# A long-convolution kernel with adapters: order of the stores and of the first tiles' moments in its preparation

## The chip, the cores and the metric

The kernel runs on one core of a Trainium2 chip. The metric is the device time of one execution in microseconds (us); three runs of the kernel before gave a median of 2400.53 us.

## The reference

The input x has 8 sequences of 2048 rows with 512 channels. Two layers follow one another, each with a layer norm in front and a residual behind:

```python
x = x + hyena(layernorm(x))      # first layer
x = x + adapters(layernorm(x))   # second layer
# hyena(x):
proj = (x @ in_proj_w + in_proj_b).reshape(B, L, C, 3)
v = depthwise_conv3(proj[..., 0], short_w) + short_b
h = gelu(pos @ fw1 + fb1); h = gelu(h @ fw2 + fb2)       # pos: 2048 positions from 0 to 1
coefs = (h @ fw3 + fb3).reshape(L, C, 2)                 # only order 1 reaches the output
conv = irfft(rfft(v, 2L) * rfft(coefs[..., 1], 2L))[:L]  # along the sequence, per channel
return (proj[..., 2] * conv) @ out_w + out_b
# adapters(x): x @ (sum over 8 ids of weight * W[id]).T, plus the mixed bias
```

The filter, that is coefs of order 1, doesn't depend on x. It is computed once and used for all 8 sequences. All is float32.

## The kernel before

The program has four stages, one behind the other, and each begins when all engines have left the stage before it. `prep` makes the filter, its partial spectrum and the split weights. `front` normalizes x, projects it and makes the first step of the transform. `middle` makes the rest of the transform, the product and the way back. `back` gates, projects and applies the adapters. The change touches `prep` alone, and beside it one more scratch slice (`fc["spare"]`, L1448).

`prep` has a program for each engine and one for the queue on SyncE (SP). They run in parallel and meet only at semaphores.

- **Loads.** SP issues 17 loads in a fixed order (L280 to L297). The small network waits for the first five of them (`net_in`), the per-row tables `ramp` and `short_w` raise `rows_in`, and `in_proj_w` comes in four blocks of 128 rows, two of them ahead and two within the loop, because `wraw` has two buffers.
- **The network.** ScalarE (ACT) and TensorE (PE) make `h2` from `pos` (L356, L416, L361). VectorE (DVE) cuts fw3 and fb3 (L488 to L493), corrects the low parts of the bias (L502, L505) and makes the running sums of `h2` by a scan (L509). PE's loop begins when it has `bias_low` from L505.
- **The first tiles' moments.** Between L493 and L502 DVE waits for x's first four tiles and makes their mean and variance (L496, L499). GpSimd (POOL) makes the factors from them with a power (L326 to L331) ahead of all its other work, and ACT normalizes tiles 0 and 1 (L371) ahead of its loop.
- **The loop.** It has iterations e = 0 to 19 for 16 tiles of 128 rows. In iteration e PE makes filter rows e (L433, L437), running sums e-1 (L447, L452) and the transform of tile e-4 (L465). DVE multiplies the filter rows by the three taps and adds them (L519, L523, L531, L536, L541). ACT copies sums e-1 to `e1` (L378) and the transform of e-4 to `s1o` (L384); in some iterations it also rounds a block of weights (L395, L396) or of the matrix (L402), whose low part POOL makes (L341, L342, L336).
- **The stores.** SP runs over tiles t, not over iterations. For each t it waits for the third tap and stores `gy` (L300), waits for the sums and stores `e1` (L302), and waits for the transform and stores `s1o` (L304). Behind tiles 1 and 3 it waits for POOL and loads a block of weights (L309).
- **The buffers.** `gy` has 4, `e1` 3, `s1o` 2, `gx` 2, `g` 5, and each of the three PSUM pairs 2. The waits on them are these:

```python
# ACT, e1_copy(t)
act.wait_ge(e1_stored[t % 3], 16 * (t // 3))   # t >= 3
# ACT, s1_copy(t)
act.wait_ge(s1_stored[t % 2], 16 * (t // 2))   # t >= 2
# DVE, third tap of tile t
dve.wait_ge(e0_stored[t % 4], 16 * (t // 4))   # t >= 4
# PE, filter_rows(e), sums(t), stage1(t)
pe.wait_ge(tap2, e - 3); pe.wait_ge(e1_done, t - 1); pe.wait_ge(s1_out, t - 1)
```

At the end SP waits for loads only, not for its last stores.

Of the kernel before, what the change touches and what calls it, by code (L numbers as in the profile page):

```python
# [10 lines left out]
ALU = mybir.AluOpType  # L11
ACT = mybir.ActivationFunctionType
# [9 lines left out]
T = 16  # L22
# [8 lines left out]
SUB = 4  # L31
# [133 lines left out]
def hyena_adapter_kernel(nc, x, in_w, in_b, short_w, short_b, fw1, fb1, fw2, fb2, fw3, fb3,  # L165
# [21 lines left out]
    def prep(fc, mc):  # L187
        with ExitStack() as st:
# [8 lines left out]
            GR = 5  # L197
            LAG = 4
            W_AT = (1, 2, 9, 12)
            W_LOAD_AT = (1, 3)  # L200
            S1_AT = (5, 6, 7, 8)
            BIAS_AT = 4

# [11 lines left out]
            pos = wide[0:64]  # L215
# [25 lines left out]
            net_in = sem("p_net_in")  # L241
# [33 lines left out]
            def edge_rows(q, t):  # L275
                return edge_f[q][:, t * C:(t + 1) * C]

            @block.sync
            def _(sp):
                sp.dma_start(w1c[:], fw1.rearrange("a (p b) -> p (a b)", b=1)).then_inc(net_in, 16)  # L280
                sp.dma_start(b1c[:], fb1.rearrange("(p b) -> p b", b=1)).then_inc(net_in, 16)
                sp.dma_start(pos, consts["pos"].partition_broadcast(64)).then_inc(net_in, 16)
                sp.dma_start(w2s[:], fw2).then_inc(net_in, 16)
                sp.dma_start(b2c[:], fb2.rearrange("(p b) -> p b", b=1)).then_inc(net_in, 16)
                sp.dma_start(b3r, fb3.rearrange("(a n) -> a n", a=1).partition_broadcast(2 * BR)).then_inc(w3_in, 16)
                sp.dma_start(w3, fw3).then_inc(w3_in, 16)
                sp.dma_start(sbr[:], short_b.rearrange("(a c) -> a c", a=1).partition_broadcast(P)).then_inc(sb_in, 16)
                for h in range(2):
                    sp.dma_start(fc["xg0"][h * N1:(h + 1) * N1], by_tile(x[0])[h, :, 0:SUB, :]).then_inc(fc["x_in"][0], 16)
                sp.dma_start(ramp, consts["ramp"].partition_broadcast(2 * BR)).then_inc(rows_in, 16)  # L290
                sp.dma_start(tapr, short_w.rearrange("(o c) a w -> o (c a w)", o=1).partition_broadcast(P)).then_inc(rows_in, 16)
                for kt in range(2):
                    sp.dma_start(wraw[:, kt], in_w[kt * P:(kt + 1) * P, :]).then_inc(w_in[kt], 16)
                sp.dma_start(s1, consts["s1"]).then_inc(mats_in, 16)
                sp.dma_start(s1x[:], consts["s1x"]).then_inc(mats_in, 16)
                sp.dma_start(bv3[:], in_b.rearrange("(a c) -> a c", a=1).partition_broadcast(P)).then_inc(mats_in, 16)
                sp.dma_start(fc["ident"][:], consts["ident"]).then_inc(mats_in, 16)  # L297
                for t in range(T):
                    sp.wait_ge(tap2, t + 1)
                    sp.dma_start(edge_rows(0, t), gy[:, t % 4]).then_inc(e0_stored[t % 4], 16)  # L300
                    sp.wait_ge(e1_done, t + 1)
                    sp.dma_start(edge_rows(1, t), e1[:, t % 3]).then_inc(e1_stored[t % 3], 16)  # L302
                    sp.wait_ge(s1_out, t + 1)
                    sp.dma_start(spec_f.rearrange("(r h t) c -> t r h c", h=2, t=T)[t], s1o[:, t % 2]).then_inc(s1_stored[t % 2], 16)  # L304
                    if t in W_LOAD_AT:

                        kt = 2 + W_LOAD_AT.index(t)
                        sp.wait_ge(w_low, 2 * (kt - 1))
                        sp.dma_start(wraw[:, kt % 2], in_w[kt * P:(kt + 1) * P, :]).then_inc(w_in[kt % 2], 16)  # L309
                sp.wait_ge(mats_in, 64)  # L310

            @block.gpsimd
            def _(pool):
                pool.memset(inside[:], 1.0 / BR).then_inc(zeroed, 1)
                pool.memset(h2[:, 0:1], 0.0).then_inc(zeroed, 1)
                pool.memset(h2[:, LP - 1:LP], 0.0).then_inc(zeroed, 1)
                pool.wait_ge(zeroed, 3)
                pool.memset(inside[:, 0, 0:1], 0.0).then_inc(zeroed, 1)
                pool.memset(inside[:, 1, P - 1:P], 0.0).then_inc(zeroed, 1)
                pool.memset(fc["power"], -0.5).then_inc(fc["power_set"], 1)  # L320
                pool.memset(fc["eps"], EPS).then_inc(fc["power_set"], 1)
                pool.memset(fc["minus"], -1.0).then_inc(fc["power_set"], 1)
                pool.wait_ge(fc["power_set"], 3)
                r, m = fc["rstd"][:, 0], fc["shift"][:, 0]
                pool.wait_ge(fc["mv_done"], SUB)
                pool.tensor_tensor(r, fc["mv"][:, 0, :, 1], fc["eps"], ALU.add).then_inc(fc["pow_step"], 1)  # L326
                pool.tensor_tensor(m, fc["mv"][:, 0, :, 0], fc["minus"], ALU.mult).then_inc(fc["pow_step"], 1)
                pool.wait_ge(fc["pow_step"], 2)
                pool.tensor_tensor(r, r, fc["power"], ALU.pow).then_inc(fc["pow_step"], 1)
                pool.wait_ge(fc["pow_step"], 3)  # L330
                pool.tensor_tensor(m, m, r, ALU.mult).then_inc(fc["norm_ready"], 1)  # L331

                def s1_lows(k):
                    part = slice(k * (T // 4), (k + 1) * (T // 4))
                    pool.wait_ge(s1_high, k + 1)
                    pool.tensor_tensor(fc["s1l"][:, part], s1[:, part], fc["s1h"][:, part].bitcast(F32), ALU.subtract).then_inc(s1_low, 1)  # L336

                def w_lows(kt):
                    rows = wraw[:, kt % 2].rearrange("p (c w) -> p c w", w=3)
                    pool.wait_ge(w_high, 2 * kt + 2)  # L340
                    pool.tensor_tensor(fc["wvl"][:, kt], rows[:, :, 0], fc["wvh"][:, kt].bitcast(F32), ALU.subtract).then_inc(w_low, 1)  # L341
                    pool.tensor_tensor(fc["wgl"][:, kt], rows[:, :, 2], fc["wgh"][:, kt].bitcast(F32), ALU.subtract).then_inc(w_low, 1)  # L342

                w_lows(0)
                w_lows(1)
                for k in range(4):
                    s1_lows(k)
                w_lows(2)
                w_lows(3)

            @block.scalar
            def _(act):
# [13 lines left out]
                        act.activation(b3ehl[:], b3e[:], ACT.Copy).then_inc(bias_high, 1)  # L366
                act.wait_ge(rows_in, 32)
                act.activation(ramp_r[:], ramp, ACT.Copy).then_inc(masks, 1)
                act.wait_ge(fc["norm_ready"], 1)
                for t in range(2):  # L370
                    act.activation(fc["xn"][:, t], fc["xg0"][:, t], ACT.Identity, bias=fc["shift"][:, 0, t:t + 1],  # L371
                                   scale=fc["rstd"][:, 0, t:t + 1]).then_inc(fc["xn_done"], 1)

                def e1_copy(t):
                    act.wait_ge(c_ps, t + 1)
# [10 lines left out]
                for e in range(T + LAG):  # L386
# [4 lines left out]
                    if e in W_AT:  # L391
                        kt = W_AT.index(e)
# [6 lines left out]
                    if e in S1_AT:  # L399
                        k = S1_AT.index(e)  # L400
                        part = slice(k * (T // 4), (k + 1) * (T // 4))
                        act.activation(fc["s1h"][:, part], s1[:, part], ACT.Copy).then_inc(s1_high, 1)  # L402
                    if e == BIAS_AT:
                        act.wait_ge(mats_in, 64)
                        bias = bv3[:].rearrange("p (c w) -> p w c", w=3)
                        act.activation(fc["bvr"][:], bias[:, 0], ACT.Copy)
                        act.activation(fc["bgr"][:], bias[:, 2], ACT.Copy)

            @block.tensor
            def _(pe):  # L410
# [75 lines left out]
            def _(dve):  # L486
# [4 lines left out]
                dve.wait_ge(sliced, 2)  # L491
                dve.tensor_tensor(b3e[:], b3s[:], sbr[0:2 * BR], ALU.mult).then_inc(sliced, 1)
                dve.tensor_tensor(w3e[:], w3s[:], sbr[:], ALU.mult).then_inc(sliced, 1)  # L493
                dve.wait_ge(fc["x_in"][0], 32)
                for i in range(SUB):
                    dve.bn_stats(fc["stats"][:, 0, i], fc["xg0"][:, i]).then_inc(fc["bn_step"], 1)  # L496
                dve.wait_ge(fc["bn_step"], SUB)
                for i in range(SUB):
                    dve.bn_aggr(fc["mv"][:, 0, i], fc["stats"][:, 0, i]).then_inc(fc["mv_done"], 1)  # L499
                low = slice(BR, 2 * BR)  # L500
                dve.wait_ge(bias_high, 1)
                dve.tensor_tensor(b3hl[low], b3s[low], b3hl[low].bitcast(F32), ALU.subtract).then_inc(bias_low, 1)  # L502
# [10 lines left out]
                for e in range(T + 2):  # L513
# [12 lines left out]
                    if e >= 2:  # L526
                        t = e - 2
# [9 lines left out]
                    if e >= 2:  # L537
                        t = e - 2
                        dve.wait_ge(tap01, t + 1)
                        dve.wait_ge(tap2, t + 1)  # L540
                        dve.tensor_tensor(g[:, t % GR], g[:, t % GR], gy[:, t % 4], ALU.add).then_inc(g_done, 1)  # L541

    def front(fc, mc):
        with ExitStack() as st:
# [888 lines left out]
    with ExitStack() as st:  # L1433
# [11 lines left out]
        fc["stats"] = small[:, 0:48].rearrange("p (s i k) -> p s i k", s=2, i=SUB)  # L1445
        fc["mv"] = small[:, 48:64].rearrange("p (s i k) -> p s i k", s=2, i=SUB)
        fc["rstd"], fc["shift"] = (small[:, 64 + 8 * k:72 + 8 * k].rearrange("p (s i) -> p s i", s=2) for k in range(2))
        fc["power"], fc["eps"], fc["minus"] = (small[:, 80 + SUB * k:80 + SUB * (k + 1)] for k in range(3))  # L1448
        for name in ("power_set", "bn_step", "mv_done", "pow_step", "norm_ready", "xn_done"):
            fc[name] = sem("f_" + name)  # L1450
        both = ExitStack()
# [62 lines left out]
```

## Time and profile before

| | |
|---|---|
| three runs | 2394.57, 2400.53, 2400.6 us |
| profiled execution | 2403.85 us |
| its span | 2402.0 us, granted clock 0.985 |
| PE busy | 2315.6 us (96%) |
| DVE busy | 1530.5 us (64%) |
| ACT busy | 843.9 us (35%) |
| POOL busy | 933.0 us (39%) |
| DMA | 496.60 MB, mean 207 GB/s |

The span is the time from the first to the last instruction, and lies 1.85 us below the device time of the same execution. The busy shares are means over all four stages. The page cuts the span in 40 slices of 60 us; the digits of PE over the first three are 6, 6 and 8, and 9 in nearly all others. `prep` takes the first 132 us. The granted clock is the share of TensorE's full clock (2.4 GHz) that a stretch had; 0.5 would be 1.2 GHz all through.

### The profile page before, as it was taken

The page shows a single profiled execution, that of the slowest core. Times are in us where ns is not written, and L with a number is a line of the kernel's source. Part 1 is how long each engine was busy: PE and PEld are TensorE (multiplying, and loading weights), DVE is VectorE, ACT ScalarE, POOL GpSimd, SP SyncE. Part 2 cuts the span into 40 slices and gives each one's busy share as a digit, 9 for nine tenths or more (in the row PEclk, how much of TensorE's full clock was granted, in tenths as well). Part 3 has the DMA queues.
Part 4 walks back from the last instruction along what each step waited for, and adds up shares of the span by engine and source line. Part 5 has one row for each costly group of instructions (what it writes and reads, how often), then busy time and mean ns, then how long its engine had stood idle before and what let it go on. Part 6 is the DMA issues. An engine that isn't in the chain of part 4 may idle for free.

```text
span 2402.0 us, 39735 instructions
## 1 busy us (share of the span) xinstructions
PE 2315.6 (96%) x12804; PEld 1624.1 (68%) x12804; DVE 1530.5 (64%) x2180; ACT 843.9 (35%) x1152; POOL 933.0 (39%) x1182
## 2 busy tenths in 40 slices
PE   6689999999999999999999979999999999999998
PEld 2267777777777777644444426777777777777776
DVE  5534444443434444367777757888888888888886
ACT  3234444444444444344444432222222222222222
POOL 2122222222222222100000026777777777777774
PEclk9889999999999999999999999999999999999999
DMA  5545545555444546589999997766665665666563
GB/s 187 181 137 159 196 140 179 162 164 196 150 162 146 188 160 221 205 312 359 356 353 355 362 358 229 246 178 176 176 180 175 179 175 176 178 179 177 177 179 101
DMA packets 180517, 496.60 MB, mean 207 GB/s; under 512 B 19419, under 2 KB 19740, under 8 KB 159332
## 3 DMA queue, kind: packets, MB, share of 16 engines
q1 hardware_dynamic: 150756, 395.10, 51.4%
q10 hardware_dynamic: 29696, 100.68, 11.6%
q8 instruction: 35, 0.57, 0.1%
q14 instruction: 30, 0.25, 0.0%
HBM read 276.27 MB, written 219.43 MB: 206 GB/s over the span
## 4 chain that ended last, share of the span: by engine, by line
PE 53%; DVE 2%; issue 2%; DMA 1%; ACT 0%; DVEq 0%; POOL 0%; POOLq 0%; SPq 0%
PE m_psW L1030 7%; PE m_psA L1013 6%; PE b_psF L183 5%; PE b_psC L1328 5%; PE b_psF L184 5%; PE b_psO L184 5%; PE b_psF L185 5%; PE b_psO L183 5%; PE b_psO L185 5%; PE b_psP L1342 2%; PE b_psT L1359 2%; DVE m_m L1101 2%; DMA spec<-wide_out 0%; DMA b_fin<-spec 0%; DVE b_o L1397 0%
## 5 line engine op out<-in xcount | busy, mean ns | idle before, releaser
L1101 DVE TENSOR_TENSOR m_m<-m_psA,m_spec 128x1024 f32<-128x1024 f32 x256 | 295.5, 1215 | 114.8 <-PE m_psA L1013 113.1
L758 POOL TENSOR_TENSOR vl<-v,vh 128x512 fp32r<-128x512 f32 x128 | 165.2, 1291 | 390.1 <-ACT vh L716 390.1
L1292 ACT ACTIVATE b_zh<-b_psT 128x512 fp32r<-128x512 f32 x128 | 76.5, 597 | 636.9 <-PE b_psT L1359 636.9
L1030 PE MATMUL m_psW<-m_m,mats 64*64 64x512 f32 x2048 | 256.0, 591 | 2.5 <-issue 2.5
L1013 PE MATMUL m_psA<-m_xin,mats 64*64 64x512 f32 x1536 | 212.9, 601 | 9.5 <-DVE m_m L1101 5.9
L183 PE MATMUL psV<-wvh,nth 128*128 128x512 f32 x512 | 213.6, 417 | 0.6 <-DVE ntl L840 0.6
L859 DVE TENSOR_TENSOR gto<-psG,bgr 128x512 f32<-128x512 f32 x128 | 87.5, 684 | 195.4 <-PE psG L185 195.2
L183 PE MATMUL b_psO<-woh,b_oh 128*128 128x512 f32 x512 | 211.8, 414 | 0.0
L183 PE MATMUL b_psF<-wfh,b_zh 128*128 128x512 f32 x512 | 207.7, 406 | 2.8 <-DVE b_zl L1421 2.8
L840 DVE TENSOR_TENSOR ntl<-psT,nth 128x512 fp32r<-128x512 f32 x128 | 88.1, 688 | 178.9 <-ACT nth L710 178.9
L184 PE MATMUL b_psO<-wol,b_oh 128*128 128x512 f32 x512 | 201.4, 393 | 0.0
L184 PE MATMUL b_psF<-wfl,b_zh 128*128 128x512 f32 x512 | 201.2, 393 | 0.0
L185 PE MATMUL b_psO<-woh,b_ol 128*128 128x512 f32 x512 | 201.2, 393 | 0.0
L184 PE MATMUL psV<-wvl,nth 128*128 128x512 f32 x512 | 201.0, 393 | 0.0
L716 ACT ACTIVATE vh<-v 128x512 fp32r<-128x512 f32 x128 | 80.9, 632 | 341.2 <-DVE v L852 341.2
L185 PE MATMUL psV<-wvh,ntl 128*128 128x512 f32 x512 | 200.6, 392 | 0.0
L185 PE MATMUL b_psF<-wfh,b_zl 128*128 128x512 f32 x512 | 200.0, 391 | 0.0
L185 PE MATMUL psG<-wgh,ntl 128*128 128x512 f32 x512 | 199.5, 390 | 0.0
L183 PE MATMUL psG<-wgh,nth 128*128 128x512 f32 x512 | 199.2, 389 | 0.0
L184 PE MATMUL psG<-wgl,nth 128*128 128x512 f32 x512 | 199.2, 389 | 0.0
L1065 ACT ACTIVATE wide_out<-m_psW 128x1024 f32<-128x1024 f32 x128 | 130.8, 1022 | 192.6 <-PE m_psW L1030 192.5
L1030 PEld LDWEIGHTS m_psW<-m_m,mats 64*64 64x64 f32 x2048 | 113.6, 134 | 111.2 <-issue 90.1
(136 smaller groups left out, 4685.3 us busy)
## 6 DMA issues: line engine op xcount, KB each, us to landing
spec<-wide_out SPq DMA_DIRECT2D x64, 1024.0 KB, 9.0
spec<-wide_out ACTq DMA_DIRECT2D x64, 1024.0 KB, 9.2
b_fin<-spec SPq DMA_DIRECT2D x128, 512.0 KB, 4.6
m_xin<-spec SPq DMA_DIRECT2D x30, 2048.0 KB, 11.7
xg<-in_L_attn_x_dram SPq DMA_DIRECT2D x64, 512.0 KB, 6.2
gate_d<-gto SPq DMA_DIRECT2D x32, 1024.0 KB, 4.0
b_gin<-gate_d SPq DMA_DIRECT2D x128, 256.0 KB, 3.6
b_xin<-in_L_attn_x_dram SPq DMA_DIRECT2D x256, 128.0 KB, 3.2
```

What stands on the lines that cost most here:

```text
L183: pe.matmul(out_ps, w_hi, d_hi, start=first, stop=False)
L184: pe.matmul(out_ps, w_hi, d_lo, start=False, stop=False)
L185: return pe.matmul(out_ps, w_lo, d_hi, start=False, stop=last)
L716: act.activation(vh[:, t % 2], v[:, t % 2], ACT.Copy).then_inc(v_hi, 1)
L758: pool.tensor_tensor(vl[:, t % 2], v[:, t % 2], vh[:, t % 2].bitcast(F32), ALU.subtract).then_inc(v_lo, 1)
L840: dve.tensor_tensor(ntl[:, t % 2], psT[t % 2][:].rearrange("p (k r) -> p k r", k=CT), nth[:, t % 2].bitcast(F32), ALU.subtract).then_inc(n ...
L859: dve.tensor_tensor(gto[:, slot, t % SUB], psG[:], bgr[:], ALU.add).then_inc(g_out, 1)
L1013: mm = pe.matmul(psA[k % RA][half[q], slot, :], w[half[slot]], xin[half[slot], par, B if k < 2 else 2 * (k - 2) + q, :], start=True, stop= ...
L1030: mm = pe.matmul(psW[pair % 2][half[slot], q, :], ws[slot][half[q]], m[half[q], pair % RM, part, slot, :], start=part == 0, stop=part == 1)
L1065: act.activation(wo[:, par, 2 * pair:2 * pair + 2, :], psW[pair % 2][:], ACT.Copy).then_inc(w_out, 1)
L1101: dve.tensor_tensor(m[:, (k - 2) % RM, part], psA[k % RA][:], spec[:, par, part], ALU.mult).then_inc(m_done, 1)
L1328: mm = pe.matmul(psC[t % 2][h * N1:(h + 1) * N1, :], s4[:, h * T + t, :], fin[:, t % 2, h, :], start=True, stop=True)
```

## The change

SP issues its stores by iteration: in iteration e the sums of tile e-1, the transform of tile e-4 and the third taps of tile e-2. The two loads of weights come behind the stores of iterations 3 and 6. `pos` is loaded ahead of `w1c` and `b1c`. The moments (DVE), their factors (POOL) and the two normalizations (ACT) stand behind all other work of their engines in `prep`. POOL makes one power on constants into a scratch slice, right behind its memsets.

```diff
-            W_LOAD_AT = (1, 3)
+            W_LOAD_AT = (3, 6)
@@ SP
+                sp.dma_start(pos, consts["pos"].partition_broadcast(64)).then_inc(net_in, 16)
                 sp.dma_start(w1c[:], ...)
                 sp.dma_start(b1c[:], ...)
-                sp.dma_start(pos, consts["pos"].partition_broadcast(64)).then_inc(net_in, 16)
...
-                for t in range(T):
+                def store_taps(t):
                     sp.wait_ge(tap2, t + 1)
                     sp.dma_start(edge_rows(0, t), gy[:, t % 4]).then_inc(e0_stored[t % 4], 16)
+                def store_sums(t):
                     sp.wait_ge(e1_done, t + 1)
                     sp.dma_start(edge_rows(1, t), e1[:, t % 3]).then_inc(e1_stored[t % 3], 16)
+                def store_spectrum(t):
                     sp.wait_ge(s1_out, t + 1)
                     sp.dma_start(spec_f..., s1o[:, t % 2]).then_inc(s1_stored[t % 2], 16)
-                    if t in W_LOAD_AT:
-                        kt = 2 + W_LOAD_AT.index(t)
+                for e in range(T + LAG):
+                    if 1 <= e <= T:
+                        store_sums(e - 1)
+                    if e >= LAG:
+                        store_spectrum(e - LAG)
+                    if 2 <= e < T + 2:
+                        store_taps(e - 2)
+                    if e in W_LOAD_AT:
+                        kt = 2 + W_LOAD_AT.index(e)
                         sp.wait_ge(w_low, 2 * (kt - 1))
                         sp.dma_start(wraw[:, kt % 2], ...).then_inc(w_in[kt % 2], 16)
@@ POOL: this is new; the factors (four operations from the wait on mv_done on) move behind w_lows(3)
+                pool.tensor_tensor(fc["spare"], fc["eps"], fc["power"], ALU.pow)
@@ ACT: from behind ramp_r to behind the loop
+                act.wait_ge(fc["norm_ready"], 1)
+                for t in range(2):
+                    act.activation(fc["xn"][:, t], fc["xg0"][:, t], ACT.Identity, ...).then_inc(fc["xn_done"], 1)
@@ DVE: from behind w3e to behind the loop
+                dve.wait_ge(fc["x_in"][0], 32)
+                for i in range(SUB):
+                    dve.bn_stats(fc["stats"][:, 0, i], fc["xg0"][:, i]).then_inc(fc["bn_step"], 1)
+                dve.wait_ge(fc["bn_step"], SUB)
+                for i in range(SUB):
+                    dve.bn_aggr(fc["mv"][:, 0, i], fc["stats"][:, 0, i]).then_inc(fc["mv_done"], 1)
```

## Rows read from the trace of the kernel before

**Rows 1.** Busy us by stretch: PE, PEld, DVE, ACT, POOL; granted clock, DMA share, GB/s

```profile
34.00:48.40 14.40, 14.22 (x59) 5.73 (x60) 14.40 (x21) 8.05 (x11) 5.13 (x4) 1.00 0.30 110
84.48:120.79 36.31, 24.53 (x75) 7.96 (x75) 20.94 (x28) 10.63 (x14) 2.80 (x2) 0.83 0.46 174
```

**Rows 2.** Longest wait of the preparation: total us, times, longest

```profile
ACT m_xin L378 <- DMA edge_f<-m_xin: 56.1, 12, 8.4
```

**Rows 3.** Timeline, one slow iteration: start us, duration, engine, line, idle before

```profile
108.69 0.60 ACT L378 ACTIVATE m_xin<-pE 128x512 f32<-128x512 f32 x1 [4.54 <-DMA edge_f<-m_xin]
109.18 1.02 ACT L384 ACTIVATE m_xin<-pS 128x1024 f32<-128x1024 f32 x1
110.22 0.55 SPq L304 DMA_DIRECT2D spec_f<-m_xin  x1
111.47 0.83 SPq L302 DMA_DIRECT2D edge_f<-m_xin  x1
114.74 0.60 ACT L378 ACTIVATE m_xin<-pE 128x512 f32<-128x512 f32 x1 [4.54 <-DMA edge_f<-m_xin]
```

**Rows 4.** Timeline, DVE's first tap in iterations 2, 5 and 7

```profile
34.00 0.88 DVE L519 TENSOR_TENSOR g<-pA,m_xin 128x512 f32<-128x512 f32 x1 [3.79 <-PE pA L437]
...
44.92 0.84 DVE L519 TENSOR_TENSOR g<-pA,m_xin 128x512 f32<-128x512 f32 x1
...
51.86 0.83 DVE L519 TENSOR_TENSOR g<-pA,m_xin 128x512 f32<-128x512 f32 x1
```

**Rows 5.** Timeline, from the network to the first iterations

```profile
7.26 2.93 ACT L356 ACTIVATE wide<-wide,b1c,w1c 64x512 f32<-64x512 f32 x4 [5.25 <-DMA b2c<-in_L_attn_fb_dram]
...
15.42 0.69 ACT L361 ACTIVATE h<-pA,b2c 128x512 f32<-128x512 f32 x1 [0.69 <-PE pA L416]
17.55 2.47 DVE L496 BATCH_NORM_STATS2 f_small<-xg 128x6 f32<-128x512 f32 x4 [3.46 <-DMA xg<-in_L_attn_x_dram]
...
21.07 0.68 DVE L505 TENSOR_TENSOR b3ehl<-b3e,b3ehl 32x512 fp32r<-32x512 f32 x1
...
21.67 1.91 ACT L368 ACTIVATE ramp_r<-wide_out 64x2048 fp32r<-64x2048 f32 x1 [5.57 <-DMA m_xin<-in_L_attn_short_w_dram]
21.78 4.42 DVE L509 TENSOR_TENSOR_SCAN wide<-h 128x2048 f32<-128x2048 f32 x1
...
27.35 1.52 ACT L371 ACTIVATE xn<-xg,f_small 128x512 f32<-128x512 f32 x2 [3.77 <-POOL f_small L331]
...
29.07 0.79 PE L452 MATMUL pE<-b3ehl,ramp_r 64*128 64x512 f32 x1
```

**Rows 6.** Timeline, last store of the preparation and first work of front

```profile
130.89 0.55 SPq L304 DMA_DIRECT2D spec_f<-m_xin  x1
...
132.13 1.94 PE L770 MATMUL psT<-fident,xn 128*128 128x128 f32 x8 [5.03 <-PEq L188]
```

**Rows 7.** Timeline, DVE, the moments of tiles 4 to 7 in front

```profile
140.48 2.46 DVE L829 BATCH_NORM_STATS2 f_small<-xg 128x6 f32<-128x512 f32 x4
143.10 0.38 DVE L836 BATCH_NORM_AGGREGATE f_small<-f_small 128x2 f32<-128x6 f32 x4 [0.15 <-DVE f_small L829]
```

**Rows 8.** Timeline, POOL, the last factor of the same tiles

```profile
145.08 0.20 POOL L754 TENSOR_TENSOR f_small<-f_small 128x4 f32<-128x4 f32 x1
```

**Rows 9.** Line L329, the first power: ns min/median/max, first and last start

```profile
L329 POOL TENSOR_TENSOR f_small<-f_small x1: 5142/5142/5142, 21.9 to 21.9; 128x4 f32<-128x4 f32 x1
```

**Rows 10.** Timeline, PE at the low clock, sums of two iterations

```profile
73.04 1.98 PE L447 MATMUL pE<-w3e,wide 128*64 128x512 f32 x4 [6.26 <-ACT m_xin L378]
...
79.58 1.91 PE L447 MATMUL pE<-w3e,wide 128*64 128x512 f32 x4
```

**Rows 11.** Line L304, all 16 stores, from issue

```profile
DMA to landing us min/median/max: 3.1/3.1/5.3
```

**Rows 12.** DVE's sum from two SBUF tiles, all 16: ns min/median/max

```profile
L536 DVE TENSOR_TENSOR g<-g,wide_out x16: 673/676/1933, 29.5 to 113.6; 128x512 f32<-128x512 f32 x16
```

**Rows 13.** POOL's low parts of the weights, four: ns min/median/max

```profile
L341 POOL TENSOR_TENSOR wvl<-wide_out,wvh x4: 1414/1438/2443, 32.2 to 99.7; 128x512 fp32r<-128x512 f32 x4
```

More of the change, by code:

```diff
@@ L323, in _ @@
                 pool.wait_ge(fc["power_set"], 3)
[L324 to L331, printed above, removed]
+                pool.tensor_tensor(fc["spare"], fc["eps"], fc["power"], ALU.pow)
                 def s1_lows(k):
@@ L349, in _ @@
                 w_lows(3)
+                r, m = fc["rstd"][:, 0], fc["shift"][:, 0]
+                pool.wait_ge(fc["mv_done"], SUB)
+                pool.tensor_tensor(r, fc["mv"][:, 0, :, 1], fc["eps"], ALU.add).then_inc(fc["pow_step"], 1)
+                pool.tensor_tensor(m, fc["mv"][:, 0, :, 0], fc["minus"], ALU.mult).then_inc(fc["pow_step"], 1)
+                pool.wait_ge(fc["pow_step"], 2)
+                pool.tensor_tensor(r, r, fc["power"], ALU.pow).then_inc(fc["pow_step"], 1)
+                pool.wait_ge(fc["pow_step"], 3)
+                pool.tensor_tensor(m, m, r, ALU.mult).then_inc(fc["norm_ready"], 1)
             @block.scalar
@@ L368, in _ @@
                 act.activation(ramp_r[:], ramp, ACT.Copy).then_inc(masks, 1)
[L369 to L372, printed above, removed]
                 def e1_copy(t):
@@ L407, in _ @@
                         act.activation(fc["bgr"][:], bias[:, 2], ACT.Copy)
+                act.wait_ge(fc["norm_ready"], 1)
+                for t in range(2):
+                    act.activation(fc["xn"][:, t], fc["xg0"][:, t], ACT.Identity, bias=fc["shift"][:, 0, t:t + 1],
+                                   scale=fc["rstd"][:, 0, t:t + 1]).then_inc(fc["xn_done"], 1)
             @block.tensor
@@ L493, in _ @@
                 dve.tensor_tensor(w3e[:], w3s[:], sbr[:], ALU.mult).then_inc(sliced, 1)
[L494 to L499, printed above, removed]
                 low = slice(BR, 2 * BR)
@@ L1447, in hyena_adapter_kernel @@
         fc["rstd"], fc["shift"] = (small[:, 64 + 8 * k:72 + 8 * k].rearrange("p (s i) -> p s i", s=2) for k in range(2))
-        fc["power"], fc["eps"], fc["minus"] = (small[:, 80 + SUB * k:80 + SUB * (k + 1)] for k in range(3))
+        fc["power"], fc["eps"], fc["minus"], fc["spare"] = (small[:, 80 + SUB * k:80 + SUB * (k + 1)] for k in range(4))
         for name in ("power_set", "bn_step", "mv_done", "pow_step", "norm_ready", "xn_done"):
```

## The prediction

> **What bounds the kernel now.** I first read the page's slices. PE is busy over 90% nearly everywhere, except in the first 130 us, and the change touches nothing else. So the question is how long the preparation lasts; from front's first matmul on, at 132.1 us [rows 6], I take the rest to shift as it is.
>
> Then I read busy time by stretch. From 34 to 48 us DVE is busy 14.40 of 14.40 us and PE 14.22: the loop is bound by its compute. From 84 to 121 us DVE has 20.94 of 36.31 us and PE 24.53, at a granted clock of 0.83 and a DMA share of 0.46 [rows 1]. So neither an engine nor the bandwidth bounds it later. The list of waits says what does: ACT's copy of the sums waits 56.1 us in 12 waits for the store of `e1` [rows 2]. One iteration of the timeline shows the ring [rows 3]: copy of the sums at 108.69, copy of the transform at 109.18, its store issued at 110.22, the store of the taps, the store of the sums issued at 111.47, and the next copy of the sums only at 114.74 when that store has landed. By the code, SP holds the sums of tile t+1 behind the transform of tile t, which PE makes four iterations later, and the copy of tile t+4 needs the same buffer. So three buffers of `e1` carry nothing: each iteration pays two copies, three issues and one landing in a row, 114.74 - 108.69 = 6.05 us.
>
> **The change, part by part.**
>
> *Stores by iteration.* The sums of tile e-1 are now issued right behind their copy, and the copy that needs that buffer comes three iterations later. Its landing after issue is 114.74 - 111.47 = 3.3 us [rows 3], against about 10 us of room. The ring is gone. What is late next is DVE, which has all its inputs in the fast stretch: first tap at 34.00 in iteration 2 and 51.86 in iteration 7 [rows 4], so 17.86 / 5 = 3.57 us an iteration, with three of POOL's operations in that stretch. At full clock PE has about the same (14.22 of 14.40 us). The next bound after these is the `s1o` pair: copy t+2 needs store t landed, so the period is at least (landing + 1.02 us of copy) / 2. Landings are 3.1, 3.1 and at most 5.3 us [rows 11], that is 2.1 to 3.2 us, under 3.57. Bandwidth: a tile stores 256 + 256 + 512 KB = 1.05 MB. 174 GB/s at share 0.46 [rows 1] is some 378 GB/s when busy, so 2.8 us for a tile. The two later loads of weights (0.79 MB, 2.1 us each) go into a slack of 16 x 0.8 = 12 us. SP's issues are about 2 us for each iteration [rows 3], also hidden. I take 3.57; bounds are 3.46 (51.86 - 44.92 over two) and about 4.5, if stores queue behind one another so that a landing takes 8 us.
>
> *Weights loaded at iterations 3 and 6.* Their waits are for POOL's low parts of blocks 0 and 1, rounded in iterations 1 and 2; the blocks are read in 9 and 12. Nothing waits: 0.
>
> *Moments taken out of the start.* DVE waited for x until 17.55 and had done L505 only at 21.75. PE's loop and the scan began on that; the network was done at 16.11 [rows 5]. Without the moments L505 ends at about 15.5, and PE and the scan start at about 16.1. Next late is `rows_in` (the tap table): ACT rounds `ramp` from 21.67 to 23.58, when that load has landed, whatever DVE does. The scan ends by then (16.1 + 4.4 = 20.5) and so do filter rows 0 and 1. So the first sums' last matmul (L452) runs at 23.6 and not at 29.07: 5.5 us earlier. DVE's iteration 2 follows it as before, at 34.00 - 5.5 = 28.5. Should PE have gone to 2.4 GHz by then, up to 2 us less; should the loads land later, up to 1 us more.
>
> *Positions first.* The network began when `b2c` had landed, at 7.26 [rows 5]; it may begin about 1.3 us earlier (two issues of 0.63 us). It ends behind `rows_in`'s load all the same: I take 0, bounds 0 and -1.3.
>
> *The first power early.* It took 5.14 us [rows 9]. Now it runs on an idle POOL before 10 us: cost 0. The later power is in the chain below at front's duration; if it should cost the first price again, +4 us.
>
> *Moments behind the loop.* DVE's loop: iteration 16 starts at 28.5 + 14 x 3.57 = 78.5. It has no first tap (2.7 us), and iteration 17 only the third tap and one sum (1.5 us): end 82.7. Now this chain is bare. Statistics and aggregation as in front, 140.48 to 143.48, are 3.0 us [rows 7]; POOL's four operations end 145.28 - 143.48 = 1.8 us later [rows 8]; ACT's two normalizations 1.5 + 0.2 us [rows 5]. That is 89.2. Beside it PE makes the last two transforms, ACT copies them and SP stores them: last g at 82.7, transform with its edge row 2 to 3 us, copy 1.0, issue 0.6, done by 87.5, so it is hidden by the chain. From the last instruction (131.44) to front's first (132.1) are 0.7 us [rows 6]. Front starts at 89.9.
>
> *Sum.* 132.1 - 89.9 = 42.2 us less. Against the profiled execution (2403.85) that is 2361.7; that execution lies 3.3 us above the median of the runs, from which I get 2358.3. I say 2359.
>
> *Shared port.* DVE is now the bound, so any delay of it counts in full. POOL has 12 operations beside the loop (8 of 1.4, 4 of 1.3 us). DVE's sum of two SBUF tiles took 0.68 us at the median and 1.93 once [rows 12]; POOL's took 2.44 once instead of 1.44 [rows 13]. The 3.57 already holds its part of that. The Trainium skill (SBUF — State Buffer, "SBUF: two separate sides") says the two engines lock one port pair for a whole instruction when DVE has two SBUF inputs, and the other blocks fully. If each POOL operation then stood in DVE's way for its length, the end would be 8 x 1.4 + 4 x 1.3 = 16.4 us later, 2375; the single maximum among 16 in rows 12 speaks against it.
>
> **The rivals.**
>
> *Landings bound the loop.* Nearly all store traffic so far came in bursts with empty time between. Sent without a pause, at 1.05 MB in 3.57 us (294 GB/s of some 378), stores may wait on one another. At a landing of 8 us the `s1o` pair gives (8 + 1.0) / 2 = 4.5 us. Where something other than DVE sets the period p, front starts at 28.5 + 15p + 1.5 + 7.2 = 37.2 + 15p: at 4.5, 104.7, so 27.4 us less and 2373. For it: the longest landing of 5.3 us came where stores were issued back to back. Against: that is still under the 6.1 us that a period of 3.57 allows. The Trainium skill (DMA: Bandwidth & Descriptors, "Latency and other measured facts") gives HBM access as 0.2 us on average and 2 us at high load; 1.8 us on top of 5.3 would be 7.1 and a period of 4.1. No row here shows a sustained load of this kind in the preparation.
>
> *The ring stays in another form.* SP still goes in order and now waits for three engines in each iteration. If that kept the period at 6.05, front would start at 128.0: 4 us less, 2396. Against: each wait is for work of the same iteration.
>
> *Slower: the low clock.* PE at 1.2 GHz needs 79.58 - 73.04 = 6.54 us for an iteration without any wait [rows 10], and it was there behind an idle time of 6.26 us. If PE's short waits kept it low through the whole loop, front would start at 37.2 + 98.1 = 135.3, 3.2 us later than now: 2404. The moments behind the loop cost here what the faster start gave, and the point of balance is a period of 6.33 us. Against: from 34 to 48 us, with the work this close together, the clock was 1.00 [rows 1]. A loss over 0.3% needs 6.8 us.
>
> **How the numbers follow.** My forecast (DVE's pace, 2359, own range 2353 to 2365) has 76%. Landings as the bound (2364 to 2380): 13%. Port lock (about 2375): 4%. The ring in another form: 3%. The low clock: 4%. The first power's price again stays in the forecast's range. The range 2352 to 2375 leaves out the last two and the ends of the others. What a measurement of this kernel can tell from no change is about 0.3%, 7 us. Faster takes the first three cases and a share of the others: 95%. Within 0.3%: 3%. Slower: 2%, from the low clock alone.
>
> **What would show it.** ACT's waits for the store of `e1` gone from the list; DVE's first taps 3.5 to 3.6 us apart from iteration 3 to 15; the granted clock near 1.00 from 30 to 80 us and DMA at about 300 GB/s there; L452 at about 23.6 and L519 of iteration 2 at 28 to 29; POOL's early power near 5 us and the late one near 1; front's first matmul at 90 us, with L371's kind last before it. I am wrong if ACT waits for the store of `s1o`, if the clock falls in the loop, or if front itself gets longer than the 2270 us between 132.1 and its end now.

## The result, and the profile after

The changed kernel takes 2358.32 us (median of 4 runs, 2356.9 to 2361.26) against 2397.65 us before (4 runs). The ratio is 0.9835, with a 95% interval of 0.9822 to 0.9847: 39.6 us less, 37 to 43 by the interval. The forecast was 2359.

The stretch table of the changed kernel, in the columns of [rows 1]:

```profile
30.00:78.00 48.00, 44.80 (x178) 17.35 (x178) 48.00 (x66) 27.18 (x36) 14.20 (x10) 1.00 0.83 298
34.00:48.40 14.40, 13.92 (x58) 5.49 (x56) 14.40 (x21) 8.99 (x13) 3.88 (x3) 1.00 1.02 330
```

Nearly the whole loop is now what the 14 us of [rows 1] were: DVE busy for 48.00 of 48.00 us, the granted clock 1.00 (2.4 GHz) throughout, and 298 GB/s.

Its list of waits in the preparation (total us, times, longest) answers to [rows 2]:

```profile
ACT m_xin L387 <- PE pE L465: 17.5, 14, 2.7
PEld pA L446 <- DVE m_xin L538: 14.0, 14, 2.0
ACT m_xin L393 <- DMA spec_f<-m_xin: 3.3, 3, 1.3
```

The 56.1 us behind the store of `e1` are gone. ACT's copy of the sums (now L387) waits for PE, its copy of the transform for a landing three times, 3.3 us in all, and PE waits for DVE's third tap (L538) in nearly every iteration. So of these DVE is last.

The timeline of the changed kernel, in the columns of [rows 3], for what answers to [rows 4 to 6]:

```profile
15.84 4.43 DVE L516 TENSOR_TENSOR_SCAN wide<-h 128x2048 f32<-128x2048 f32 x1 [1.62 <-ACT h L374]
19.75 1.91 ACT L381 ACTIVATE ramp_r<-wide_out 64x2048 fp32r<-64x2048 f32 x1 [3.95 <-DMA m_xin<-in_L_attn_short_w_dram]
22.73 0.50 PE L465 MATMUL pE<-b3ehl,ramp_r 64*128 64x512 f32 x1
25.61 0.88 DVE L526 TENSOR_TENSOR g<-pA,m_xin 128x512 f32<-128x512 f32 x1 [1.43 <-PE pA L450]
28.84 1.95 DVE L548 TENSOR_TENSOR g<-g,m_xin 128x512 f32<-128x512 f32 x1
30.72 0.85 DVE L526 TENSOR_TENSOR g<-pA,m_xin 128x512 f32<-128x512 f32 x1
34.19 0.85 DVE L526 TENSOR_TENSOR g<-pA,m_xin 128x512 f32<-128x512 f32 x1
37.67 0.89 DVE L526 TENSOR_TENSOR g<-pA,m_xin 128x512 f32<-128x512 f32 x1
...
66.29 1.94 DVE L548 TENSOR_TENSOR g<-g,m_xin 128x512 f32<-128x512 f32 x1
...
68.14 0.84 DVE L526 TENSOR_TENSOR g<-pA,m_xin 128x512 f32<-128x512 f32 x1
...
82.17 0.69 DVE L548 TENSOR_TENSOR g<-g,m_xin 128x512 f32<-128x512 f32 x1
82.78 2.46 DVE L551 BATCH_NORM_STATS2 f_small<-xg 128x6 f32<-128x512 f32 x4
85.13 1.02 ACT L393 ACTIVATE m_xin<-pS 128x1024 f32<-128x1024 f32 x1 [1.56 <-PE pS L481]
86.16 1.02 POOL L360 TENSOR_TENSOR f_small<-f_small 128x4 f32<-128x4 f32 x1
87.50 1.52 ACT L419 ACTIVATE xn<-xg,f_small 128x512 f32<-128x512 f32 x2 [1.34 <-POOL f_small L362]
89.32 1.94 PE L783 MATMUL psT<-fident,xn 128*128 128x128 f32 x8 [4.23 <-PEq L188]
```

DVE's iteration 2 begins at 25.61 and not at 34.00. Nine of the twelve steps between first taps from iteration 3 to 15 are 3.45 to 3.50 us; the others are 3.9, 4.0 and, from 12 to 13, 5.2. From iteration 2 to 3 it is 5.1. In the two long steps a sum took 1.95 us. DVE leaves its loop at 82.86. The last transform is copied at 86.15; the normalizations end at 89.02 and are last. Front's first matmul is at 89.32, against 132.13 in [rows 6]: 42.8 us earlier. Front lasts 877.7 us (877.3 before).

### The profile page after: what moved, and what is told of

It reads as the page before. It is cut to its first block, busy times and chain, and to the rows that moved or that the text cites. A ratio compares the mean times of both kernels' runs of the same rounds, so it can differ in the third digit from the quotient of the medians.

```text
span 2356.3 us, 39735 instructions
## 1 busy us (share of the span) xinstructions
PE 2299.8 (98%) x12804; PEld 1620.2 (69%) x12804; DVE 1530.4 (65%) x2180; ACT 845.5 (36%) x1152; POOL 930.3 (39%) x1183
## 4 chain that ended last, share of the span: by engine, by line
PE 54%; DVE 2%; issue 2%; DMA 1%; ACT 0%; DVEq 0%; POOL 0%; POOLq 0%; SPq 0%
PE m_psW L1043 7%; PE m_psA L1026 6%; PE b_psF L183 6%; PE b_psC L1341 5%; PE b_psF L184 5%; PE b_psO L184 5%; PE b_psO L183 5%; PE b_psO L185 5%; PE b_psF L185 5%; PE b_psP L1355 2%; PE b_psT L1372 2%; DVE m_m L1114 2%; DMA spec<-wide_out 0%; DMA b_fin<-spec 0%; DVE b_corr L1405 0%
```

## The experiments

Front's first matmul is the mark in all that follows, since the preparation ends there. Times with an interval are ratios to the kernel before, run on the same chip beside it.

**Stores alone, moments alone.**

```diff
# e1_order_only: the kernel before, plus this part of the change alone (in short)
-    W_LOAD_AT = (1, 3); for t in range(T): taps(t); sums(t); spectrum(t)
+    W_LOAD_AT = (3, 6); for e in range(T + LAG): sums(e-1); spectrum(e-4); taps(e-2)
# e2_moments_only: the kernel before, plus the moves on DVE, POOL and ACT and the early power
```

> The kernel before with the stores by iteration and the two later loads of weights at iterations 3 and 6; positions, moments, factors and first normalizations stay where they were, and there is no early power. Theory (the stores' order frees the ring, DVE's pace is the next bound): DVE's first tap of iteration 2 stays at 34.0, the loop takes the 57.3 us that it takes in the changed kernel, DVE ends at 91.3, and front's first matmul is at 95.8: 36 us less than before, about 2361 to 2364 us. Rival (the gain needs the earlier start, since stores and late loads of the start collide): the period stays above 4.5 us and front starts later than 110.

> The kernel before with only the moments, factors and normalizations behind the loop and the early power; stores by tile and positions third, as before. Theory: the loop's first full iteration comes 5.5 to 8 us earlier, the ring of 6.05 us stays, the moments on DVE are hidden beside the last ring turns, only the two normalizations (1.5 us) stand behind ACT's last copy. Front's first matmul is at 125 to 128, 4 to 7 us less than before. Rival (moments behind the loop cost their whole chain of 6.4 us there as well): front at 131 to 133, no gain.

The stores alone gave 2361.43 us, ratio 0.9851 (0.9834 to 0.9869), 36 us less. The moments alone gave 2394.81 us, ratio 0.9986 (0.9974 to 0.9998), some 3 us less. The timelines of the two, the first kernel first, and for the second also its longest wait for a store in the preparation:

```profile
26.27 0.53 PE L449 MATMUL pA<-b3hl,inside_r 64*128 64x512 f32 x1
...
92.64 1.94 PE L782 MATMUL psT<-fident,xn 128*128 128x128 f32 x8 [2.32 <-PEq L188]
```

```profile
ACT m_xin L375 <- DMA edge_f<-m_xin: 55.8, 12, 7.8
```

```profile
22.50 1.91 ACT L369 ACTIVATE ramp_r<-wide_out 64x2048 fp32r<-64x2048 f32 x1 [6.23 <-DMA m_xin<-in_L_attn_short_w_dram]
...
125.63 1.02 ACT L381 ACTIVATE m_xin<-pS 128x1024 f32<-128x1024 f32 x1 [1.74 <-DMA spec_f<-m_xin]
126.55 1.50 ACT L407 ACTIVATE xn<-xg,f_small 128x512 f32<-128x512 f32 x2
...
128.88 1.94 PE L771 MATMUL psT<-fident,xn 128*128 128x128 f32 x8 [4.66 <-PEq L188]
```

With the stores alone front starts at 92.6, better than the 95.8 expected: DVE's iteration 2 began at 30.7 and not at 34.0, and its loop took 57.4 us, as expected. The bias matmul of iteration 1 took 0.53 us, against 0.79 in the kernel before, so PE worked at the high clock earlier. With the moments alone the ring stays (55.8 us in 12 waits for the store of `e1`, against 56.1 in 12 in [rows 2]), and the normalizations stand bare behind ACT's last copy. Front at 128.9 misses the 125 to 128 expected; the tap table landed 0.8 us later here (22.50) than in [rows 5]. The rival of e1 falls: the stores' order alone carries nine tenths of the gain, and the tenth that is left lies within the intervals of the two ratios.

**The positions' place.**

```diff
# e3_pos_back: the changed kernel with
- loads in the order pos, w1c, b1c, w2s, b2c
+ loads in the order w1c, b1c, pos, w2s, b2c
```

> The changed kernel with the positions' load back in third place. In the changed kernel ACT's rounding of ramp, which waits for the tap table, began at 19.75 and not at 21.67. Theory A (the order of the loads moved that landing): it is at 21.5 again, the first sums are 1.9 us later, and front's first matmul comes at 91.2. Theory B (that landing differs from run to run, or the moments' move did it): it stays near 19.8 and front's first matmul at 89.3 to 89.6.

The tap table's wait ended at 20.42, and front started at 90.1; one run took 2359.56 us. The network began at 7.19. In all traces of this case it began at 7.14 to 7.42 with positions third (six traces) and at 6.04 to 6.96 with positions first (seven). So the new place gives the network about 0.6 us by the medians (7.30 and 6.70), and in single traces up to the 1.3 us of the forecast's bound. In e3 the network is 0.2 us later than in the changed kernel, and DVE's iteration 2 begins 0.4 us later (25.98). Neither theory's number came out; the repeats below show that the landing differs from run to run.

**The early power.**

```diff
# e4_no_early_power: the changed kernel with
-    pool.tensor_tensor(fc["spare"], fc["eps"], fc["power"], ALU.pow)
# e8_early_power_old_place: e1_order_only with
+    pool.tensor_tensor(fc["spare"], fc["eps"], fc["power"], ALU.pow)
```

> The changed kernel without the early power on constants. Theory A (the first power of a program costs 5.1 us, as the prediction read it): the power behind the loop takes 5.1 us instead of 1.02, and front's first matmul comes at 93.4. Theory B (in the kernel before the power stood beside DVE's scan from 21.8 to 26.2 and waited for it; the early power took only 1.04 us in the changed kernel): the power behind the loop takes 1.0 us and front stays at 89.3.

> The first experiment's kernel (stores by iteration alone; the factors stand ahead of POOL's other work, where the power ran from 21.7 to 26.9 beside DVE's scan) with the early power on constants added. Theory (the power waits for DVE's scan): it still takes 5.1 us and ends 0.9 us behind the scan. Rival (the first power of a program costs 5.1 us): the early one takes that, and the later one 1.0.

Without the early power, POOL's timeline behind the loop:

```profile
85.74 1.03 POOL L359 TENSOR_TENSOR f_small<-f_small 128x4 f32<-128x4 f32 x1
```

With it, and the factors at their old place, DVE and then POOL:

```profile
19.85 4.42 DVE L522 TENSOR_TENSOR_SCAN wide<-h 128x2048 f32<-128x2048 f32 x1
```

```profile
19.96 5.13 POOL L342 TENSOR_TENSOR f_small<-f_small 128x4 f32<-128x4 f32 x1
```

Front starts at 88.9 in e4, as its second theory had it. The first power of a program costs 1.03 us. The one of 5.14 us in [rows 9] cost that because it stood beside the scan: here it starts 0.1 us behind the scan's start and ends 0.8 us behind its end, although another power had run before (at 1.6 us, 1.04 us long). In the four traces with the factors at their old place it takes 5.13 to 5.14 us and begins 0.1 us behind the scan's start, whether that is at 19.8 or at 21.8. The two kernels took 2356.67 and 2359.98 us in one run each. The early power is worth nothing.

**Who sets the pace.**

```diff
# e5_dve_extra: the changed kernel, in iterations 1 to 16, with (its semaphore left out here)
+    dve.tensor_tensor(spare_t[:], w3s[:], w3e[:], ALU.add)
# e6_taps_stored_twice: the changed kernel with (the waits on e0_stored count twice as much)
+    sp.dma_start(edge_2[:, t * C:(t + 1) * C], gy[:, t % 4]).then_inc(e0_stored[t % 4], 16)
```

> The changed kernel with one more DVE addition of two SBUF tiles (0.6 us from start to start) in each of iterations 1 to 16. Theory (DVE sets the loop's pace now): all of it shows, so the first taps are 4.1 us apart, front's first matmul comes 15 x 0.6 = 9 us later, at 98.3, and the time is 2367. Rival (PE or the landings set it, DVE only looks full): DVE takes the addition in its waits, front stays before 92.

> The changed kernel with each tile of third taps stored twice, the second time into a scratch tensor of its own: 1.31 MB a tile instead of 1.05, 22.5 MB in the loop with the weights. Theory (DMA has little room left): at the 385 GB/s seen in bursts that is 58.5 us against a loop of 57.3, so landings grow, ACT waits for the store of s1o in most iterations, and front comes 2 to 5 us later, at 91 to 94. Rival (DMA has ample room): unchanged, 89.3. Second rival (the two buffers of s1o bind at once): a period of over 4 us, front after 97.

With DVE's extra addition, its timeline:

```profile
52.62 0.83 DVE L528 TENSOR_TENSOR g<-pA,m_xin 128x512 f32<-128x512 f32 x1
...
56.69 0.83 DVE L528 TENSOR_TENSOR g<-pA,m_xin 128x512 f32<-128x512 f32 x1
```

4.07 us an iteration instead of 3.48; front at 97.5, 8.2 us later; 2365.41 us, ratio 0.9863 (0.9847 to 0.9880). DVE sets the pace, and the rival falls.

With the taps stored twice, its stretch, the wait for `s1o`'s store and that store's landings:

```profile
30.00:78.00 48.00, 45.40 (x182) 17.41 (x178) 48.00 (x65) 27.02 (x36) 18.10 (x10) 1.00 0.99 367
```

```profile
ACT m_xin L395 <- DMA spec_f<-m_xin: 18.0, 10, 3.6
```

```profile
DMA to landing us min/median/max: 3.1/5.2/7.9
```

The DMA is full (share 0.99, 367 GB/s), landings grow to 5.2 us at the median, and ACT waits 18.0 us for them. But DVE stays at 48.00 of 48.00 us, front starts at 88.8, and the time is 2359.17 us, ratio 0.9837 (0.9820 to 0.9853): unchanged. ACT has 27 us of work in 48, and `g` has five buffers; that these take in the waits is read from the code and wasn't tried by itself. The theory's mechanism showed and its price didn't.

**Moments in DVE's gap.**

```diff
# e7_moments_in_gap: the changed kernel with the blocks that the change moved behind the loops at
+ DVE: behind iteration 1; POOL: behind w_lows(1); ACT: in iteration 10
```

> The changed kernel with the moments on DVE behind iteration 1, the factors on POOL behind the low parts of weight blocks 0 and 1, and the two normalizations on ACT in iteration 10. In the changed kernel DVE waits 1.4 us for the filter rows of iteration 2. Theory: the moments' 2.9 us cost 1.5 us there, the chain behind the loop goes, and the last transform, its copy and its store end the preparation 4.5 us behind DVE: front's first matmul at 82.9 + 1.5 + 4.5 = 88.9, 0.4 us earlier than now, which no measurement tells apart. Rival (the moments delay the taps by their full length and PE goes down to 1.2 GHz while it waits): front at 91 to 95.

The end of its preparation:

```profile
85.21 1.68 PE L479 MATMUL pS<-g,wide_out 64*128 64x512 f32 x4 [0.41 <-DVE g L549]
85.89 4.62 SPq L308 DMA_DIRECT2D spec_f<-m_xin  x2
86.82 2.07 PE L482 MATMUL pS<-g_before,ps1x 1*128 1x512 f32 x2
88.92 1.02 ACT L393 ACTIVATE m_xin<-pS 128x1024 f32<-128x1024 f32 x1 [3.06 <-PE pS L482]
```

DVE left the loop at 85.2, 2.3 us later than with the moments behind it: its iteration 2 began 0.7 us later, and its sums took 1.6 us more than in the changed kernel, so the moments' own price here is nearer to 0.7 than to the 1.5 expected. The tail was 1.6 us longer than expected, for PE was down to the low clock in the last transform (granted clock 0.55 from 85 to 91 us): its last four matmuls took 1.68 us and not 1.13, its edge row 2.07 and not 1.12. Front at 91.2; the time, 2357.58 us, ratio 0.9827 (0.9811 to 0.9844), can't be told from the changed kernel's. The rival's sign is the nearer one, with another place for the low clock. Behind the loop is as good a place as this.

**The shared port.**

```diff
# e11_no_lows: the changed kernel with POOL's 12 low parts as
+    pool.memset(<the same tile>, 0.0)
```

> The changed kernel with POOL's 12 low parts left out: each is a fill with zeros of the same tile, which reads no SBUF (so the low parts of the weights and of the matrix are missing from the products). In the changed kernel DVE's two sums of SBUF tiles took 4.5 us more than their usual 0.67 each, in two traces 4.5 and 3.1, always beside a low part; the prediction charged DVE's pace of the fast stretch, which holds about 0.4 us of this. Theory (the shared port costs that): no such sum takes over 0.75 us, all first taps from iteration 3 on are 3.5 us apart, and front's first matmul comes 3 to 4.5 us earlier, at 85 to 86. Rival (PE at 3.5 us an iteration takes up the slack): the sums are short but front stays at 89.

Its second sum of two SBUF tiles, and then the same in the changed kernel (ns, min/median/max):

```profile
L548 DVE TENSOR_TENSOR g<-g,m_xin x16: 671/690/771, 27.5 to 77.2; 128x512 f32<-128x512 f32 x16
```

```profile
L548 DVE TENSOR_TENSOR g<-g,m_xin x16: 666/692/1952, 28.8 to 82.2; 128x512 f32<-128x512 f32 x16
```

The maximum falls from 1.95 to 0.77 us (0.75 was expected), and DVE's first taps from iteration 3 on are 3.5 us apart. Front starts at 84.8, 4.5 us earlier, and the time is 2352.64 us, ratio 0.9815 (0.9797 to 0.9832; this interval and the changed kernel's just overlap). The rival falls. But not all of the 4.5 us is the port's. DVE's iteration 2 began at 24.53 and not at 25.61, 1.1 us earlier. From there to the loop's end it was 53.4 us, against 57.3 in the changed kernel's trace and 55.9 in its repeat: the low parts cost 3.9 or 2.5 us. The tail was 0.5 us longer. The fills are also shorter than the low parts (0.53 us, not 1.3 to 1.4), which this run doesn't separate from their reading nothing. In the changed kernel's trace all six sums of over 0.8 us stand beside a low part, and the taps, which read PSUM, stay at 0.80 to 0.90 us beside one.

The Trainium skill (SBUF — State Buffer, "SBUF: two separate sides") describes an exclusive lock on a shared port pair between a DVE operation with two SBUF inputs and a GpSimd operation that reads SBUF: whoever starts first keeps the other out for its whole length. The traces agree: the longest sum takes 1.95 us, its own 0.67 and some 1.3 of a low part, and the power above ends 0.8 us behind the scan beside it.

**Both kernels once more.**

> The kernel before, unchanged, profiled once more. Two things in the traces so far are unexplained: the tap table's load landed at 21.7, 21.6 and 22.5 in three kernels and at 19.8 to 20.5 in seven others, and the middle stage lasted 420.8 us in the two kernels with stores by tile, where PE paused 2.2 to 2.5 us early in it, and 415.4 to 417.5 us in the eight with stores by iteration. If both belong to the kernel, this trace shows a landing near 21.7, the pause, and 420.8 us. If they differ from run to run, either may move by 1 us or more.

> The changed kernel, unchanged, profiled once more, for the same two questions. If both belong to the kernel: landing at 19.8, no pause, a middle stage of 416 to 417 us, front's first matmul at 89.3. If they differ from run to run, the landing or the middle stage moves by 1 us or more.

The kernel before, in its second trace:

```profile
129.38 0.87 PE L770 MATMUL psT<-fident,xn 128*128 128x128 f32 x3 [3.88 <-PEq L188]
```

There the tap table's wait ended at 19.74, 1.9 us before that of [rows 5]; the middle stage lasted 417.3 us instead of 420.8, and PE's pause was 1.5 us. The changed kernel repeated itself: wait's end at 19.86, front at 89.2, middle 415.9. So landing and middle stage differ by some us from run to run, and of the 45.7 us between the two first spans (2402.0 and 2356.3) some 4 belong to the run of before that was profiled. The second pair has 129.4 - 89.2 = 40.2 us in the preparation, and spans of 2397.0 and 2355.7, 41.3 us apart. From front's first matmul to the end it is 2269.9 and 2267.0 us in the first pair, 2267.6 and 2266.4 in the second.

## Why the prediction was right, and where its terms were not

*The ring.* Right, and shown: with the stores' order alone the wait for `e1` goes and 36 us with it; without it the moments' move leaves the ring as it was. DVE was next, as forecast; e5 shows it.

*The start.* Forecast 5.5 us, in the first pair of traces 34.00 - 25.61 = 8.4. One part of the difference is a bound of the term come true, the other wasn't in it: from the sums' last matmul to DVE's iteration 2 it was 2.9 us instead of 4.9, for PE was already at 2.4 GHz (the matmul took 0.50 us; 0.79 in [rows 5]), and that matmul ran at 22.73 and not at 23.6. `rows_in` landed 1.9 us earlier, where the forecast had only a later landing as a bound. Of that only 0.9 us came through: ACT had rounded `ramp` at 21.66, and the matmul then stood behind PE's own work, without a pause from 15.86 on. So with an early landing it is the network and PE that set the start, and not the table. The granted clock is 1.00 for all these stretches in both traces and doesn't show the step; the durations do, 1.98 us for four filter matmuls up to 18.5 us and 1.13 from 23.2 on, and up to 29.8 and from 34.1 on in the kernel before. The landing isn't the change's doing. In the second pair, with equal landings, DVE's iteration 2 began at 30.76 and 26.60: 4.2 us.

*The loop.* Forecast 28.5 to 82.7, 54.2 us; measured 25.61 to 82.86, 57.3, and 55.9 in the repeat. The mis-sized term is the pace of 3.57 us, taken to hold its part of the shared port. All 32 sums together took 4.5 us more than 0.67 us each (3.1 in the repeat), 1.9 in the kernel before, and 1.4 without low parts (e11). So the port's part in the sums is 3.1 us in the changed kernel (1.7 in the repeat) and 0.5 in the kernel before. There nine of the twelve low parts also ran while DVE was at work, but mostly beside taps: beside sums they stood for 3.6 us in all, in the changed kernel for 7.5. The price that the port rival was refused for "the single maximum among 16" was between: 2.5 to 3.9 us of loop (e11), not 0.4 and not 16.4. With DVE always busy each low part finds it at work, but only a sum beside it pays. Apart from that the pace was 3.48.

*The tail.* Forecast 7.2 us from DVE's end to front, measured 6.5, in the order forecast: statistics, factors, normalizations. The last transform ended 2.9 us before the normalizations.

Front's start at 89.3 (forecast 89.9) came out because the start was 2.9 us better and the loop 3.1 us worse than forecast. The mechanism was right, but two of the sum's terms cancelled, and that is luck. A second pair cancelled in the time: the forecast took 42.2 us off a median of 2400.5. With four runs that median is 2397.65, and the change gave 39.3 us less than it. Both are 2.9 us smaller than assumed, so the time came out though the saving didn't. The saving by the forecast was 42.2 us; by the second pair of traces it was 40.2 us in the preparation and 1.2 us behind it.

*The signs.* Held: no wait for the store of `e1`, the clock, 298 GB/s, front at 89.3 with the normalizations last. Not held: three of the twelve steps from iteration 3 to 15 were 3.9 to 5.2 us, the sums' last matmul and DVE's iteration 2 came earlier than said, and the early power took 1.04 us and not 5. One sign of being wrong came too: ACT did wait for the store of `s1o`, 3.3 us in three waits. DVE was busy for 48.00 of 48.00 us all the same, so that sign was too strict: a wait says nothing until it reaches the engine that is last.

*The moments' move* is worth little alone. Front starts at 91.0 in e8 and at 89.3 in the changed kernel, with landings at 19.9 and 19.75: 1.7 us. Against the kernel before, e2 starts front 3.2 us earlier than its first trace and 0.5 us earlier than its second. About 3 us at the start are given back in part as the longer tail (4.6 us from DVE's end in e8, 6.5 here). The forecast had 5.5 minus about 2.7.

*The first power.* The reading of [rows 9] as a price of the first use was wrong (e4, e8); what the power paid for was the scan beside it. The cost forecast, zero, came out because the power no longer stands beside the scan.

*Landings as the bound.* The rival's mechanism is real when the DMA is full (e6: longest landing 7.9 us), but its formula, (landing + copy) / 2, needs every landing to be that long; the median of 5.2 gives 3.1 us, under DVE's pace. In the changed kernel the landings were 3.1, 3.5 and at most 6.9 us (min, median, max).

*The low clock* as the slower case didn't come: 1.00 from 30 to 78 us.

What stays open: why the first landing and PE's pause early in the middle stage differ between runs. In the traces with stores by iteration the middle stage lasted 415.4 to 417.5 us, in three with stores by tile 420.8, 420.9 and 417.3; whether anything of this follows from the change isn't settled.

## What to carry to other kernels

A queue that takes its work tile by tile, while the engines make the parts of a tile in different iterations, puts the youngest store behind the oldest, and the buffers of the early parts stop working as buffers. Issue by iteration, in the order in which the results come. When a loop turns from waiting to busy, price again every side operation that can hold up the bound engine: here the sums lost 0.5 us beside a loop that waited and 1.7 to 3.1 beside one that didn't, where 16.4 us was the price if every low part had stood in the way. An unusually long small operation is first compared with what runs beside it on the other engines, before it is called a first-use cost.

## What the hardware showed beside the question

POOL's power on 128x4 elements took 5.13 us beside DVE's scan of 4.42 us over SBUF, and 1.03 us alone, whether first or not. Stores of 2 KB rows and two loads of weights held 367 GB/s at a DMA share of 0.99 for 48 us, and DVE was busy for all of them, as without the added stores.
